# Sorted experts: back transfers issued twelve iterations ahead, a group of results every two and a half blocks

## The chip, the core and the metric

The kernel runs on one core of a Trainium2 chip. Its engines are TensorE (PE: matmuls and transposes, PEld its weight loads), VectorE (DVE), ScalarE (ACT), GpSimd (POOL) and SyncE (SP, which here only issues transfers). Each runs its own instructions in the order of its program and waits on semaphores for the others. The metric is the device time in microseconds; lower is better. A profiled execution gives a trace of one run.

## What is computed

A decoder layer for 64 sequences of 128 tokens of width 128, in f32: linear attention, attention over a context of 120 tokens, and a mixture of experts, each followed by a normalisation. The change lies in the third part:

```python
logits = x @ gate_w.T;  scores = softmax(logits)
topk_w, topk_i = top_k(scores, 2)
topk_w = topk_w / (topk_w.sum(-1) + 1e-20) * 2.5
...
g = silu(x @ w_gate[e]) * (x @ w_up[e])        # 8 experts, width 176
y = sum over the token's two experts of  topk_w * (g @ w_down[e])
y = y + (silu(x @ sw_gate) * (x @ sw_up)) @ sw_down     # shared expert, width 352
x = layernorm(x + y)
```

## The kernel before

During the second part the tokens' rows are sorted by expert into `sorted_rows` in device memory, once for sequences 0 to 47 and once for 48 to 63 (`PER = (48, 16)`). The last stage, `experts` (line 1420), then works through `TOTAL` = 142 blocks of 128 sorted rows, 103 of the first batch (`FIRST_BLOCK[1]` = 103) and 39 of the second. It is one loop over iterations t, which each engine's program runs through for itself; block i passes through it in stages:

- TensorE transposes the rows of block t (`turn_rows`), multiplies block t-1 with its expert's gate and up weights (`gate_up`), transposes the hidden rows of t-2 and projects t-3 down.
- ScalarE casts the transposed rows (`hi`), applies silu (`gate`) and copies hidden rows out (`turn`).
- VectorE forms the low part (`lo` of t), the product with the row's weight (`product` of t-1) and copies the result of t-3 out (`take`).
- GpSimd scatters the result of block t-3 into `sorted_results` in device memory, each row to its token's place (`scatter`, line 1595).
- SyncE loads the rows of blocks, three blocks at a time (`load_rows`): at its iteration t (a multiple of 3) those of blocks t+12 to t+14. For that it waits until the results of blocks t to t+2 have been scattered and landed, since the rows' buffers also hold the scatter's indices. `x_rows` (in the trace `w_wkv`) has 12 buffers. The last rows are loaded in iteration 129.

The shared expert is worked into the same loop for 16 groups of four sequences, in eight pieces a group from iteration 8 on; piece 0 to 2 of a group are its gate and up products, pieces 3 to 6 its projections. Groups 14 and 15 come after the blocks, from iteration 143 on, in seven pieces each (`LATE_FROM = TOTAL + 1`). `add_shared` adds a group's result to its rows in `X`.

When all blocks of the first batch are scattered, the results of its tokens can be fetched back: groups g = 0 to 11 (`WHOLE` = 12) while blocks 103 to 141 still run, groups 12 to 15 after the last block. `BACK_TIME[g]` is the iteration of a group's addition, and all its steps stand relative to it (first number for g < 12, second for the others):

- `load_back`: two transfers of 256 KB (a token's two expert results) into one of five `back` buffers, at -5 on SyncE. It waits for the sum of group g-5 (`BACKS` = 5). For g = 12, 13 it is at iteration `TOTAL + 5` on SyncE, for g = 14, 15 at `TOTAL + 11` on ScalarE, each behind a wait for the last scatter (`sent_after`).
- `add_pair` (line 1602), GpSimd, at 0: waits for both transfers and adds the two halves.
- `add_back` (line 1749), VectorE, at +1: waits for `add_pair` and `add_shared`, adds `X`, starts the statistics; `moments` at +2 ends them.
- `root` (line 1609), GpSimd, at +4 or +3; `shifts`, VectorE, at +5 or +4.
- `normalise` (line 1665), ScalarE, at +6 and +7, or +5 and +6: two activations each into one of four `result` buffers (`DEEP` = 4); the first waits until the store of group g-4 has landed.
- `store` (line 1549), SyncE, at +8 or +7: 256 KB to the output.

What sets the order is therefore the iteration in which a step is written; within an iteration an engine does its block's work first, and GpSimd the scatter, then `root`, then `add_pair`. SyncE does `load_rows`, then `load_back`, then `store`.

Of the kernel before, what the change touches and what calls it, by code (L numbers as in the profile page):

```python
# [155 lines left out]
FIRST_BLOCK = [sum(BLOCKS[:n]) for n in range(BATCHES + 1)]  # L156
TOTAL = FIRST_BLOCK[BATCHES]
# [7 lines left out]
GROUPS = B // GROUP  # L165
# [1254 lines left out]
def experts(nc, X, ident, later, slots, out):  # L1420
# [11 lines left out]
    LATE = 2  # L1432
    LATE_FROM = TOTAL + 1
    WHOLE = FIRST[1] // GROUP
    BACK_TIME = [FIRST_BLOCK[1] + 9 + 3 * g if g < WHOLE else TOTAL + 13 + 2 * (g - WHOLE) for g in range(GROUPS)]
    STEPS_ALL = BACK_TIME[-1] + 9
    CLOSE_AT = 30
    TABLE_AT = 10
# [3 lines left out]
    with ExitStack() as stack:  # L1442
# [72 lines left out]
        def prepared_at(t):  # L1515

            starts = [SHARED_FROM + PIECES * g for g in range(GROUPS)]
            return starts.index(t) if t in starts else None

        def back_at(t, *delays):  # L1520

            for g, start in enumerate(BACK_TIME):
                if t - start == delays[g >= WHOLE]:
                    return g
            return None

        @block.sync
        def _(sp):
# [24 lines left out]
            for t in range(STEPS_ALL):  # L1553
                if t % SET == 0 and t + RING < TOTAL:
                    load_rows(t // SET + LOADS)
                g = prepared_at(t + 13)
                if g is not None and g > 1:
                    load_all(g)
                if t == CLOSE_AT:
                    sp.wait_ge(slots.empty_ready, 6)  # L1560
                    sp.wait_ge(slots.table_ready, TABLE + 2)
                    slots.close_regions(sp, empty, 1)
                g = back_at(t, -5, -5)
                if g is not None and g < WHOLE:
                    if g == 0:
                        sent_after(sp, FIRST_BLOCK[1])
                    for c in range(2):
                        load_back(sp, g, c)
                if t == TOTAL + 5:
                    sent_after(sp, TOTAL)  # L1570
                    for g in (WHOLE, WHOLE + 1):
                        for c in range(2):
                            load_back(sp, g, c)
                g = back_at(t, 8, 7)
                if g is not None:
                    store(g)
# [49 lines left out]
        def _(act):  # L1626
# [42 lines left out]
            for t in range(STEPS_ALL):  # L1669
                if t < TOTAL:  # L1670
                    hi(t)
                if 0 <= t - 1 < TOTAL:
                    gate(t - 1)
                if 0 <= t - 2 < TOTAL:
                    turn(t - 2)
                g, k = shared_at(t)
                if g is not None and k < NS:
                    all_gate(g, k)
                g = prepared_at(t + 2)
                if g is not None:  # L1680
                    all_hi(g)
                if t == 1:
                    slots.turned_rows(act, ps_s, LAST)
                if t == 3:
                    slots.scores_of(act, LAST)
                for pair in range(2):
                    g = back_at(t, 6 + pair, 5 + pair)
                    if g is not None:
                        normalise(g, pair)
                if t == TOTAL + 11:  # L1690
                    sent_after(act, TOTAL)
                    for g in (WHOLE + 2, WHOLE + 3):
                        for c in range(2):
                            load_back(act, g, c)
# [237 lines left out]
```

## Time and profile before

| | |
|---|---|
| median of 3 runs | 2119.89 us (2117.36 to 2120.77) |
| profiled execution, whole | 2114.67 us |
| its span in the trace | 2112.9 us |
| TensorE busy over the span | 1958.9 us, 93% |
| VectorE, ScalarE, GpSimd busy | 72%, 60%, 63% |
| `experts`, first scatter to end of span | 1704.1 to 2112.9 us |
| additions of groups (`add_pair`) | 16, from 1969.6 to 2103.4 us |
| granted TensorE clock, whole span | 0.97 of full speed |

The shares are means over stages that differ. TensorE is over 90% busy up to the stretch in which the groups are added, and 50 to 60% in the last tenth of the span, so that stretch is read by itself: by the list of waits, and by the instructions in order of time, on each engine. A time in brackets behind an instruction is how long its engine stood idle before it, with the instruction or transfer that ended the wait.

### The profile page before, as it was taken

Reading aid. Unit: us, or ns where it says so; the run is one execution under the profiler, and the core shown is the slowest. Engines: PE = TensorE matmul, PEld = TensorE weight load, DVE = VectorE, ACT = ScalarE, POOL = GpSimd, SP = SyncE. Lnnn points to the kernel's source line nnn. Section 1 sums busy time; section 2 is a strip of 40 time slices with the busy share of each in tenths; the row PEclk is TensorE's granted clock in tenths of the full one; section 3 lists DMA queues with packets and bytes.
Section 4 is the critical chain, followed back from the end, with each engine's and each line's share of the span. In section 5 each row is a group of like instructions: output and inputs, shape, how many; then the busy total and the mean of one; then the engine's idle time right before and its main releaser. Section 6 shows DMA issues by size and latency. Waiting matters only on the chain. (4 is left out here: it accounts for less than half of the span.)

```text
span 2112.9 us, 47421 instructions
## 1 busy us (share of the span) xinstructions
PE 1958.9 (93%) x15991; PEld 1703.1 (81%) x15991; DVE 1527.1 (72%) x4046; ACT 1259.4 (60%) x3812; POOL 1336.8 (63%) x1459
## 2 busy tenths in 40 slices
PE   6888859999999999999999999999999999999655
PEld 4555449999999999999999999998999878888544
DVE  5999956777777777777777777778777655555445
ACT  3565536666666666666666666666666544444334
POOL 5899937666666666666666666666666654444445
PEclk9999979999999999999999999999999989999867
DMA  4200000000000000000000000001000122222335
GB/s 135 63 18 18 16 25 6 9 21 17 16 14 21 15 16 15 20 15 18 15 16 20 17 16 14 21 17 35 15 19 16 39 58 81 78 73 71 87 87 158
DMA packets 105022, 75.78 MB, mean 36 GB/s; under 512 B 11044, under 2 KB 98676, under 8 KB 104660
## 3 DMA queue, kind: packets, MB, share of 16 engines
q1 hardware_dynamic: 93732, 53.66, 9.1%
q0 software_dynamic: 8640, 17.97, 2.5%
q8 instruction: 135, 2.21, 0.4%
q10 hardware_dynamic: 2416, 1.12, 0.2%
q14 instruction: 99, 0.81, 0.1%
HBM read 40.15 MB, written 32.57 MB: 34 GB/s over the span
## 5 line engine op out<-in xcount | busy, mean ns | idle before, releaser
L1026 POOL TENSOR_TENSOR x_prob<-x_prob,x_inv 128x496 f32<-128x496 f32 x514 | 521.7, 1015 | 459.6 <-DVE x_inv L1176 457.0
L1104 ACT ACTIVATE x_prob<-x_ps_S,x_nmax 128x248 f32<-128x248 f32 x1028 | 472.8, 467 | 225.6 <-DVE x_nmax L1170 223.7
L1170 DVE TENSOR_REDUCE x_nmax<-x_ps_S 128x2 f32<-128x496 f32 x515 | 344.9, 670 | 105.1 <-PE x_ps_S L848 97.0
L1118 ACT COPY x_probT<-x_ps_T 124x512 f32<-124x512 f32 x512 | 300.3, 587 | 166.7 <-PE x_ps_T L1358 164.0
L846 PE MATMUL x_ps_S<-x_kT_lo,x_G_hi 128*128 128x248 f32 x1030 | 328.6, 319 | 0.0
L1358 PE MATMUL x_ps_T<-ident,x_prob 128*124 128x128 f32 x2048 | 319.0, 278 | 7.9 <-POOL x_prob L1026 6.4
L1358 PEld LDWEIGHTS x_ps_T<-ident,x_prob 128*124 128x124 f32 x2048 | 233.1, 140 | 74.1 <-POOL x_prob L1026 30.3
L848 PE MATMUL x_ps_S<-x_kT_hi,x_G_hi 128*128 128x248 f32 x1030 | 285.9, 278 | 0.0
L847 PE MATMUL x_ps_S<-x_kT_hi,x_G_lo 128*128 128x248 f32 x1030 | 285.5, 277 | 0.0
L1328 PE MATMUL x_ps_O<-x_probT,x_V 124*64 124x128 f32 x4096 | 251.9, 276 | 0.4 <-ACT x_probT L1118 0.4
L1595 POOL DMA_INDIRECT sorted_results<-e_y,w_wkv x142 | 149.2, 1051 | 158.9 <-DVE e_y L1719 149.2
L1156 DVE TENSOR_TENSOR x_G_lo<-x_ps_G,x_G_hi 128x512 fp32r<-128x512 f32 x259 | 177.9, 687 | 89.3 <-ACT x_G_hi L1098 89.1
L1328 PEld LDWEIGHTS x_ps_O<-x_probT,x_V 124*64 124x64 f32 x4096 | 221.0, 137 | 18.9 <-issue 5.2
L1104 ACT ACTIVATION_READ_ACCUMULATOR x_prob<-x_ps_S,x_nmax 128x1 f32 x1028 | 206.9, 201 | 0.0
L1098 ACT CAST x_G_hi<-x_ps_G 128x512 fp32r<-128x512 f32 x259 | 152.4, 589 | 74.5 <-PE x_ps_G L848 73.9
L847 PEld LDWEIGHTS x_ps_S<-x_kT_hi,x_G_lo 128*128 128x128 f32 x1030 | 195.7, 190 | 0.0
L846 PEld LDWEIGHTS x_ps_S<-x_kT_lo,x_G_hi 128*128 128x128 f32 x1030 | 194.8, 189 | 0.0
L848 PEld LDWEIGHTS x_ps_S<-x_kT_hi,x_G_hi 128*128 128x128 f32 x1030 | 194.1, 188 | 0.0
L1162 DVE COPY x_V<-x_ps_V 124x512 f32<-124x512 f32 x259 | 175.5, 678 | 2.6 <-PE x_ps_V L848 2.6
L281 POOL DMA_INDIRECT sorted_rows<-w_rows,slots_slot x128 | 132.3, 1034 | 27.9 <-issue 23.5
L847 PE MATMUL x_ps_G<-x_kT_hi,x_M_lo 128*128 128x256 f32 x518 | 146.3, 282 | 0.0
L846 PE MATMUL x_ps_G<-x_kT_lo,x_M_hi 128*128 128x256 f32 x518 | 146.0, 282 | 0.1
(240 smaller groups left out, 4491.1 us busy)
## 6 DMA issues: line engine op xcount, KB each, us to landing
w_wkv<-sorted_rows SPq DMA_DIRECT2D x142, 66.0 KB
e_back<-sorted_results SPq DMA_DIRECT2D x28, 256.0 KB, 3.5
x_nk<-latents SPq DMA_DIRECT2D x34, 124.0 KB
latents<-lin_nlat SPq DMA_DIRECT2D x32, 128.0 KB, 1.8
turned_rows<-w_rows SPq DMA_DIRECT2D x32, 128.0 KB, 1.7
w_wq<-turned_rows SPq DMA_DIRECT2D x32, 128.0 KB
out_dram<-e_result SPq DMA_DIRECT2D x16, 256.0 KB, 2.4
x_nk<-in_ctx SPq DMA_DIRECT2D x34, 120.0 KB, 2.3
```

The lines of the kernel that those rows point to most:

```text
L846: nc.tensor.matmul(out, stationary[0], moving[1], start=first, stop=False)
L847: nc.tensor.matmul(out, stationary[1], moving[0], start=False, stop=False)
L848: return nc.tensor.matmul(out, stationary[0], moving[0], start=False, stop=last)
L1026: nc.gpsimd.tensor_tensor(prob[:, k], prob[:, k], inv[:, k].unsqueeze(2).broadcast_to([P, 2, K]), ALU.mult).then_inc(prob_ready, 1)
L1098: nc.scalar.copy(G_part[0][:, pair], ps_G[:]).then_inc(G_hi_ready, 1)
L1104: nc.scalar.activation(prob[:, k, h, :], ps_S[:, n % BANKS, h * K:(h + 1) * K], ACT.Exp, bias=nmax[:, k, h:h + 1], accum_out=total[:, k, h ...
L1118: nc.scalar.copy(probT[0:KT, s % (2 * GANG)], ps_T[0:KT, s % 2, :]).then_inc(probT_ready, 1)
L1156: nc.vector.tensor_tensor(G_part[1][:, pair].rearrange("p h u q -> p (h u q)"), ps_G[:], G_part[0][:, pair].bitcast(F32).rearrange("p h u ...
L1162: nc.vector.tensor_copy(V[:, hf, u, tile, :], ps_V[0:KT, :]).then_inc(V_ready, 1)
L1170: nc.vector.tensor_reduce(nmax[:, k, :], ps_S[:, n % BANKS, 0:2 * K].rearrange("p (h k) -> p h k", h=2), AX, ALU.max, negate=True).then_in ...
L1328: last = nc.tensor.matmul(ps_O[h * DH:(h + 1) * DH, k * S:(k + 1) * S], V[:, j // 4, u, tile, (j % 4 * 2 + h) * DH:(j % 4 * 2 + h + 1) * D ...
L1358: last = nc.tensor.transpose(ps_T[0:KT, s % 2, at:at + S], prob[:, s % RINGS, h, tile * KT:(tile + 1) * KT], ident[:])
```

## The change

Four numbers change. `BACK_TIME` of the first twelve groups begins at iteration 115 instead of 112 and goes on by 2.5 iterations instead of 3 (115, 117, 120, 122, ... 142 instead of 112, 115, ... 145). That of the last four is 152, 154, 156, 158 instead of 155, 157, 159, 161. The transfers of the first twelve are issued twelve iterations ahead instead of five, so in SyncE's iterations 103, 105, 108, ... 130 instead of 107, 110, ... 140. ScalarE's transfers for groups 14 and 15 move from iteration 153 to 148. All steps that stand relative to `BACK_TIME` move with it. The loop ends after 167 iterations instead of 170.

```diff
-    BACK_TIME = [FIRST_BLOCK[1] + 9 + 3 * g if g < WHOLE else TOTAL + 13 + 2 * (g - WHOLE) for g in range(GROUPS)]
+    AHEAD = 12
+    BACK_TIME = [FIRST_BLOCK[1] + AHEAD + 5 * g // 2 if g < WHOLE else TOTAL + 10 + 2 * (g - WHOLE) for g in range(GROUPS)]
...
-                g = back_at(t, -5, -5)
+                g = back_at(t, -AHEAD, -AHEAD)
                 if g is not None and g < WHOLE:
...
-                if t == TOTAL + 11:
+                if t == TOTAL + 6:
                     sent_after(act, TOTAL)
```

GpSimd, around the first four additions, before. `sorted_results` is the scatter of a block, `e_back` the addition of a group, `e_rstd` its root:

```order
 L1595 DMA sorted_results<-e_y,w_wkv 20224x128 x104
 L1602 TENSOR_TENSOR e_back<-e_back 128x512
 L1595 DMA sorted_results<-e_y,w_wkv 20224x128 x3
 L1602 TENSOR_TENSOR e_back<-e_back 128x512
 L1595 DMA sorted_results<-e_y,w_wkv 20224x128
 L1609 TENSOR_TENSOR e_rstd<-e_vare,slots_half 128x4
 L1595 DMA sorted_results<-e_y,w_wkv 20224x128 x2
 L1602 TENSOR_TENSOR e_back<-e_back 128x512
```

The same place in the changed program (line numbers are one higher):

```order
 L1596 DMA sorted_results<-e_y,w_wkv 20224x128 x107
 L1603 TENSOR_TENSOR e_back<-e_back 128x512
 L1596 DMA sorted_results<-e_y,w_wkv 20224x128 x2
 L1603 TENSOR_TENSOR e_back<-e_back 128x512
 L1596 DMA sorted_results<-e_y,w_wkv 20224x128 x2
 L1610 TENSOR_TENSOR e_rstd<-e_vare,slots_half 128x4
 L1596 DMA sorted_results<-e_y,w_wkv 20224x128
 L1603 TENSOR_TENSOR e_back<-e_back 128x512
 L1596 DMA sorted_results<-e_y,w_wkv 20224x128
 L1610 TENSOR_TENSOR e_rstd<-e_vare,slots_half 128x4
```

The first addition stands three scatters later, and between two additions there are two and three scatters in turn instead of three.

SyncE, around the first store (of group 0), before. `w_wkv` are the rows of a block (here the last of three), `e_back` a group's pair of back transfers, `out_dram` a group's store:

```order
 L477 DMA w_wkv<-sorted_rows 128x132
 L1549 DMA out_dram<-e_result 128x4x128
 L1501 DMA e_back<-sorted_results 128x4x128 x2
 L476 TENSOR_LOAD slots_row_of
 L476 ISA x2
 L477 ISA
 L477 DMA w_wkv<-sorted_rows 128x132
```

The same place in the changed program:

```order
 L477 DMA w_wkv<-sorted_rows 128x132
 L1502 DMA e_back<-sorted_results 128x4x128 x2
 L1550 DMA out_dram<-e_result 128x4x128
 L1502 DMA e_back<-sorted_results 128x4x128 x2
 L1550 DMA out_dram<-e_result 128x4x128
 L476 TENSOR_LOAD slots_row_of
```

The store of group 0 was directly behind the rows of iteration 120; now it is in iteration 123, behind that iteration's rows and the pair of group 8, and the store of group 1 follows behind another pair ahead of the next rows.

VectorE, behind its last product of the shared expert (`e_all_hidden`), before. `e_hsum` is a group's sum, `e_stat`, `e_mom`, `e_vare` its statistics, `X` the last `add_shared`:

```order
 L1734 TENSOR_TENSOR e_all_hidden<-e_all_silu,e_ps_up 96x512
 L1749 TENSOR_TENSOR e_hsum<-e_back,X 128x512
 L1753 BN_STATS e_stat<-e_hsum 128x6 x2
 L1742 TENSOR_TENSOR X<-X,e_ps_s 128x512
 L1758 BN_STATS e_stat<-e_hsum 128x6 x2
 L1761 BN_AGGR e_mom<-e_stat 128x2 x4
 L1764 TENSOR_SCALAR e_vare<-e_mom 128x4
 L1749 TENSOR_TENSOR e_hsum<-e_back,X 128x512
```

The same place in the changed program:

```order
 L1735 TENSOR_TENSOR e_all_hidden<-e_all_silu,e_ps_up 96x512
 L1750 TENSOR_TENSOR e_hsum<-e_back,X 128x512
 L1754 BN_STATS e_stat<-e_hsum 128x6 x2
 L1759 BN_STATS e_stat<-e_hsum 128x6 x2
 L1762 BN_AGGR e_mom<-e_stat 128x2 x4
 L1765 TENSOR_SCALAR e_vare<-e_mom 128x4
 L1750 TENSOR_TENSOR e_hsum<-e_back,X 128x512
 L1754 BN_STATS e_stat<-e_hsum 128x6 x2
 L1759 BN_STATS e_stat<-e_hsum 128x6 x2
 L1762 BN_AGGR e_mom<-e_stat 128x2 x4
 L1765 TENSOR_SCALAR e_vare<-e_mom 128x4
 L1770 SCALAR_TENSOR_TENSOR e_shift<-e_mom,e_rstd 128x4
```

The last `add_shared` stood between the halves of group 12's statistics; now the whole of groups 12 and 13 stands ahead of it.

## Rows read from the trace of the kernel before

**Rows 1.** List of waits, 1680 us to the end: waiter <- awaited: us, times, longest.

```profile
PE e_ps_x L1808 <- DVE e_xT_lo L1703: 51.7, 25, 7.0
DVE e_hsum L1749 <- POOL e_back L1602: 45.0, 12, 6.4
POOL e_back L1602 <- DMA e_back<-sorted_results: 43.9, 11, 6.2
```

**Rows 2.** GpSimd in order of time: start, duration (us), line, out<-in, [idle before].

```profile
1969.61 1.26 POOL L1602 TENSOR_TENSOR e_back<-e_back 128x512 f32<-128x512 f32 x1 [5.79 <-DMA e_back<-sorted_results]
...
2018.98 1.42 POOL L1595 DMA_INDIRECT sorted_results<-e_y,w_wkv  x1 [0.16 <-issue]
...
2023.86 0.97 POOL L1595 DMA_INDIRECT sorted_results<-e_y,w_wkv  x1 [1.15 <-DVE e_y L1719]
2029.47 1.25 POOL L1602 TENSOR_TENSOR e_back<-e_back 128x512 f32<-128x512 f32 x1 [4.64 <-DMA e_back<-sorted_results]
...
2072.62 1.29 POOL L1602 TENSOR_TENSOR e_back<-e_back 128x512 f32<-128x512 f32 x1
...
2076.77 1.03 POOL L1595 DMA_INDIRECT sorted_results<-e_y,w_wkv  x1 [0.20 <-issue]
2078.10 0.97 POOL L1595 DMA_INDIRECT sorted_results<-e_y,w_wkv  x1 [0.30 <-issue]
2079.10 1.29 POOL L1602 TENSOR_TENSOR e_back<-e_back 128x512 f32<-128x512 f32 x1
```

**Rows 3.** Groups of instructions, 1968 to 2073 us: busy, mean ns, idle before.

```profile
L1602 POOL TENSOR_TENSOR e_back<-e_back 128x512 f32<-128x512 f32 x10 | 12.6, 1259 | 41.7 <-DMA e_back<-sorted_results 41.7
```

**Rows 4.** All engines in order of time: a block's first transpose, and one `take`.

```profile
1955.22 0.27 PE L1808 MATMUL e_ps_x<-ident,w_wkv 128*128 128x128 f32 x1
...
1957.35 0.29 DVE L1719 COPY e_y<-e_ps_y 128x128 f32<-128x128 f32 x1 [0.58 <-PE e_ps_y L1832]
...
1961.72 0.27 PE L1808 MATMUL e_ps_x<-ident,w_wkv 128*128 128x128 f32 x1
...
1964.69 0.28 PE L1808 MATMUL e_ps_x<-ident,w_wkv 128*128 128x128 f32 x1
...
2011.51 0.42 PE L1808 MATMUL e_ps_x<-ident,w_wkv 128*128 128x128 f32 x1
...
2013.88 0.42 PE L1808 MATMUL e_ps_x<-ident,w_wkv 128*128 128x128 f32 x1
```

**Rows 5.** Stretches: length, busy PE, PEld, DVE, ACT, POOL, then granted clock, DMA, GB/s.

```profile
2006.50:2011.00 4.50, 2.03 (x8) 1.80 (x9) 3.29 (x16) 0.68 (x3) 3.76 (x4) 0.50 0.05 16
...
2077.00:2084.00 7.00, 5.72 (x28) 3.81 (x26) 4.91 (x18) 4.05 (x9) 6.28 (x6) 1.00 0.22 69
2084.00:2098.00 14.00, 10.73 (x66) 8.27 (x66) 6.90 (x22) 6.13 (x15) 6.12 (x6) 1.00 0.67 196
```

**Rows 6.** SyncE's issues in order of time: rows of blocks, first store, pair of transfers.

```profile
2022.40 2.60 SPq L477 DMA_DIRECT2D w_wkv<-sorted_rows  x3
2025.04 0.43 SPq L1549 DMA_DIRECT2D out_dram<-e_result  x1
2025.52 1.12 SPq L1501 DMA_DIRECT2D e_back<-sorted_results  x2
```

**Rows 7.** From issue to landing: first the back transfers, then the stores.

```profile
DMA to landing us min/median/max: 2.8/3.6/5.2
...
DMA to landing us min/median/max: 2.2/2.4/5.0
```

**Rows 8.** ScalarE: first half of `normalise` of group 3, in iteration 127.

```profile
2022.61 0.88 ACT L1665 ACTIVATE e_result<-e_hsum,e_shift,e_rstd 128x128 f32<-128x128 f32 x2
```

**Rows 9.** VectorE in order of time, near the end.

```profile
2094.27 0.68 DVE L1749 TENSOR_TENSOR e_hsum<-e_back,X 128x512 f32<-128x512 f32 x1
...
2097.38 0.69 DVE L1742 TENSOR_TENSOR X<-X,e_ps_s 128x512 f32<-128x512 f32 x1 [1.91 <-PE e_ps_s L1859]
...
2104.69 0.69 DVE L1749 TENSOR_TENSOR e_hsum<-e_back,X 128x512 f32<-128x512 f32 x1
```

## The prediction, made before the changed kernel was run

> **What bounds the kernel now.** The list of waits comes first, for the last 430 us: I looked for one wait that three engines share. VectorE's sum of a group waits 45.0 us for GpSimd's addition of the two halves, in 12 waits; that addition itself waits 43.9 us for the transfer from `sorted_results`, in 11; and TensorE's transposes wait 51.7 us for VectorE [rows 1]. It is one queue of waits: the transfer is late, GpSimd stands, VectorE stands behind it in program order, so `lo` of the next block is late and TensorE runs dry.
>
> Next GpSimd in order of time [rows 2]. The addition of g = 0 stands 5.79 us, that of g = 5 4.64 us; of the ten additions up to 2073 nine stand so (g = 0 to 8), together 41.7 us [rows 3]. From 2072.62 on nothing stands: there the transfers were issued after SyncE's last rows of blocks, and GpSimd works without a gap. That stretch shows the next limit.
>
> Why the transfers are late, although issued "five iterations ahead": SyncE is not at the iteration of the others. `load_rows` at its iteration t waits until the scatter of block t+2 has landed, which GpSimd issues at t+5. So the transfer issued at 2025.52 belongs to the addition at 2029.47 [rows 2, 6], with no lead: the wait is its landing (2.8 to 5.2 us) [rows 7].
>
> Last the clock. In a stretch after a stall the granted clock is 0.50 (1.2 GHz), in stretches where TensorE is 77 to 82% busy it is 1.00 (2.4 GHz) [rows 5]. A block takes 2.37 us at the low level, TensorE without a gap (2011.51 to 2013.88) [rows 4].
>
> **The change, part by part.** *Transfers twelve iterations ahead.* The instructions are the same ones. Seven iterations more, at the 2.37 us of a block, are 16.6 us of lead against the 5.2 us of the longest landing. The waits of g = 0 to 8 go; what they cost is not their sum, since GpSimd then has less slack and the clock differs, so I build the new stretch up from its start.
>
> *Start.* Iterations 113 and 114 take 2.97 us each as before (1961.72 to 1964.69); iteration 115 starts at 1967.7. Its `take` follows 2.1 us later (1955.22 to 1957.35), the scatter some 0.6 us after that and lasts about 1 us, so the addition of g = 0, now in iteration 115, starts at about 1971.4 [rows 4].
>
> *Pace.* What is next late is GpSimd itself. From one addition to the next over three iterations it needs 6.48 us (2072.62 to 2079.10): addition, three scatters, one root [rows 2]. Over two iterations one scatter of 1.33 us goes (2076.77 to 2078.10): 5.2 us. TensorE needs at most 2.37 us for a block [rows 4], 5.9 us for the 2.5 blocks of a group even at the low clock, beside GpSimd's mean of 5.8. The additions stand in iterations 115, 117, 120, ... 142: five long gaps and six short, of which the first has no root and takes 5.2 - 1.2 = 4.0 us, two blocks of TensorE at some 2 us each. Sum: 5 x 6.48 + 5 x 5.2 + 4.0 = 62.4 us. Bounds: the scatter behind an addition takes 1.42 us and others 0.97 [rows 2]; were all eleven short, 5 us less (57.4). Were each block 2.6 us (the 2.37 of a low clock and some of VectorE's wait), 27 blocks are 70 us. I take 62.4, since its rows are the same instructions in the same order.
>
> *A new wait.* `normalise(g + 4)` overwrites the result buffer of g and waits for its store. It now stands 16 iterations behind BACK_TIME of g, before 18, while the store stays at +8 in SyncE's program, and SyncE is late as shown. The store of g = 0 is at SyncE's iteration 123, behind that iteration's rows and a pair of back transfers. From GpSimd's scatter of iteration 128: 3.42 us until SyncE passes its gate (2018.98 to 2022.40), 2.64 for three rows, 1.1 for the pair (rows of 1.12), then landing, 2.4 (median) to 5.0 us: 9.6 to 12.2 us [rows 2, 6, 7]. ScalarE reaches `normalise(4)` (iteration 131) 1.25 us before GpSimd's scatter there (2022.61 against 2023.86), so 6.48 - 1.25 = 5.2 us on that scale [rows 2, 8]. It waits 4.4 to 7.0 us. Behind it on ScalarE are `hi` of block 132 and `gate`, for which VectorE, TensorE and GpSimd wait: from the landing to the next scatter 2.4 us (two normalisations, `hi`, `lo`, `product`, `take`), so that scatter comes at 12.0 to 14.6 instead of 9.2: 2.8 to 5.5 us lost. I take 4. The store of g = 1 lands 1.6 us later and is wanted two iterations later: no wait. Those of g = 2 and 3 fall within 1 us of their need, and from g = 4 on SyncE has no gate. Below: 0, if the store's landing is shorter or blocks slower; above: 12, if three of the four wait.
>
> The store shares SyncE's queue with two 256 KB transfers just ahead of it. The Trainium skill (DMA: Bandwidth & Descriptors, section on queues, rings and completion order) says that one DMA engine takes a queue's descriptors in their order; by that the landing would be nearer 5.0 than 2.4 us, and the loss 5.5 rather than 2.8. No row before has a store directly behind such a pair with its own landing beside it.
>
> *Stretch of blocks together.* The addition of iteration 142 was at 2079.10; it comes at 1971.4 + 62.4 + 4 = 2037.8: 41.3 us earlier.
>
> *Tail.* From that addition to the end the order is nearly the old one. Before, VectorE ends its products at 2094.27, starts g = 12, waits 1.91 us for TensorE's last projection (2097.38), and only then does g = 12's rest and g = 13, until g = 15's sum at 2104.69 [rows 9]. Now g = 12 and 13 stand ahead of that wait and fill it: 2 us less. ScalarE's four transfers now stand ahead of the last gates: 4 issues of some 0.5 us, but the normalisations of g = 11 that stood there in part are done earlier; nothing either way. Bounds: -4 (the rest of the chain is also VectorE's) and +2 (the issues delay the gates). I take -2.
>
> *Edits at nothing:* transfers for g = 0 to 3 fall into iterations 103 to 112; SyncE has idle time there and their rows are wanted more than five iterations later. The five back buffers: the transfer of g waits for the sum of g - 5, 11.5 iterations ahead of its own addition; SyncE comes there some seven ahead. If SyncE were not gated, it would wait an iteration and a half.
>
> **Sum.** 41.3 + 2 = 43.3 us. The profiled execution took 2114.67 us (span 2112.9 and 1.8 around it); it would take 2071.4. The three timed runs have their median at 2119.89, 5.2 above; I count from the median: 2119.9 - 43.3 = 2076.6, so 2077 us. Extremes: 57.4, no store wait, -4 give 2066; 70, 12, +2 give 2096.
>
> **Rivals.**
> *The clock stays low.* GpSimd as the bound leaves TensorE idle for a part of every group; for it: behind a stall the clock was still 0.50 during the next blocks. Against it: 1.00 at 77% busy [rows 5]. Then the pace is the 70 us of above: 2084; with another store wait 2090. The Trainium skill (TensorE: Matmul & The Clock Gate, section "A second HAM failure mode: psum-queue depth-cycling") tells of a kernel whose clock swings because of frequent short idles; by that rule it would come out so.
> *No store wait.* If the first store lands within 5 us of SyncE's gate, or blocks are slower there, the 4 us stay: 2073.
> *Several store waits* (three at 4 us): 2085.
> *It does not do what it says.* If SyncE stood more than 12 iterations behind, the transfers would still be waited for: 2120. Against it: the gate is at five iterations and landing.
> *Slower: SyncE becomes the bound.* Between two gates it issues three rows (2.6 us), 1.2 pairs and 1.2 stores. If rows land late, TensorE starves in every third block. Before, three blocks took 109.5 / 10 = 10.9 us (addition 0 to 10); the kernel gets slower once SyncE needs more than that per three blocks, for instance 11.3: 2124. Its rows give 2.64 + 1.2 x (1.12 + 0.43) = 4.5 us [rows 6].
>
> **How the numbers follow.** Forecast (one store wait, GpSimd's pace, 2075 to 2080) 0.60; low clock 0.14; several store waits 0.08; no store wait or scatters all short (2066 to 2073) 0.12; no effect 0.03; slower 0.03. Predicted 2077. The range of 8 in 10 leaves out the last two, the slowest part of the low clock and the fastest of the fourth: 2068 to 2091. A measurement of this kernel tells 0.2%, some 4 us, from no change. Faster 0.94, same 0.03, slower 0.03.
>
> **What the new profile would show.** Right: no wait of the additions for the transfer until g = 11; GpSimd at 5.8 us a group and over 85% busy in iterations 117 to 142; the clock at 1.00 there; one idle stretch of ScalarE of 4 to 7 us ahead of a normalisation of g = 4; the pieces of g = 13 ahead of the last `add_shared`. Wrong: the additions still stand; the clock's mean in that stretch under 0.8; TensorE or VectorE without a gap while GpSimd waits; rows of blocks waited for by TensorE. The least certain steps are the pace and the size of the store wait.

## The result

The changed kernel takes 2084.47 us (median of 4 runs, 2082.94 to 2085.23) against 2119.72 us of the kernel before in the same session (median of 4): ratio 0.9834, 95% interval 0.9817 to 0.9851. That is 35.3 us less, inside the range and 7.5 us above the 2077 predicted. The profiled execution of the changed kernel took 2083.88 us (span 2081.9).

The line numbers after the change are one higher. In these first lines (list of waits, 1680 us to the end: waiter <- awaited: us, times, longest), those that answer to [rows 1] are the first three:

```profile
PE e_ps_x L1809 <- DVE e_xT_lo L1704: 18.3, 25, 5.0
POOL e_back L1603 <- DMA e_back<-sorted_results: 8.7, 2, 6.1
DVE e_hsum L1750 <- POOL e_back L1603: 7.2, 7, 2.1
ACT e_result L1666 <- DMA out_dram<-e_result: 5.9, 2, 5.1
```

The queue of waits is gone: 43.9 us in 11 waits of GpSimd for the transfers are now 8.7 in 2, TensorE's 51.7 us are 18.3. The last line is new: ScalarE waits for a store, as forecast.

GpSimd of the changed kernel in order of time, answering to [rows 2] (start, duration, line, out<-in, [idle before]): the additions of g = 0, 6, 10, 11, 12 and 13, and between them what follows on that of g = 6:

```profile
1977.23 1.29 POOL L1603 TENSOR_TENSOR e_back<-e_back 128x512 f32<-128x512 f32 x1
...
2010.65 1.19 POOL L1596 DMA_INDIRECT sorted_results<-e_y,w_wkv  x1 [1.09 <-DVE e_y L1720]
...
2016.35 1.29 POOL L1603 TENSOR_TENSOR e_back<-e_back 128x512 f32<-128x512 f32 x1
2017.81 1.43 POOL L1596 DMA_INDIRECT sorted_results<-e_y,w_wkv  x1 [0.17 <-issue]
2019.26 1.04 POOL L1610 TENSOR_TENSOR e_rstd<-e_vare,slots_half 128x4 f32<-128x4 f32 x1
2023.39 1.03 POOL L1596 DMA_INDIRECT sorted_results<-e_y,w_wkv  x1 [3.09 <-DVE e_y L1720]
...
2045.41 1.29 POOL L1603 TENSOR_TENSOR e_back<-e_back 128x512 f32<-128x512 f32 x1
2050.62 1.30 POOL L1603 TENSOR_TENSOR e_back<-e_back 128x512 f32<-128x512 f32 x1
2062.94 1.29 POOL L1603 TENSOR_TENSOR e_back<-e_back 128x512 f32<-128x512 f32 x1 [6.08 <-DMA e_back<-sorted_results]
2066.86 1.27 POOL L1603 TENSOR_TENSOR e_back<-e_back 128x512 f32<-128x512 f32 x1 [2.63 <-DMA e_back<-sorted_results]
```

No addition up to g = 11 stands. Those of g = 12 and 13, whose transfers can only start behind the last block, still do. The addition of g = 11 (iteration 142) is at 2050.62; the forecast on the scale of the profile of before was 2037.8. Here the two executions have to be laid side by side with care. SyncE's first pair of back transfers, the first instruction that the change moves, is at 1962.81 us after. A scatter of GpSimd well ahead of it (iteration 99, below called the common scatter) is at 1933.15 us before and the same one at 1938.20 after, and the rows that SyncE issues behind it at 1933.26 and 1938.31. The 5.0 us between them belong to the executions, not to the change: the profiled execution of before was 5.2 us under its own median. Counted from there, the addition of iteration 142 is 7.8 us later than forecast, and the rest is in these stretches (length, busy PE, PEld, DVE, ACT, POOL, granted clock, DMA share, GB/s; each from one addition to the next, the last is all eleven):

```profile
1981.74:1989.82 8.08, 6.23 (x34) 4.11 (x33) 7.44 (x25) 3.54 (x11) 5.52 (x5) 1.00 0.38 110
...
2016.35:2024.45 8.10, 3.10 (x16) 2.40 (x15) 3.44 (x14) 2.64 (x9) 4.78 (x4) 0.85 0.76 221
2024.45:2032.98 8.53, 7.82 (x37) 7.15 (x37) 6.49 (x24) 4.71 (x16) 5.50 (x5) 0.55 0.50 143
...
2045.41:2050.62 5.21, 4.74 (x28) 3.80 (x27) 4.10 (x17) 4.02 (x11) 4.79 (x4) 0.96 0.25 77
```

```profile
1977.23:2050.62 73.39, 55.27 (x289) 45.15 (x289) 52.40 (x203) 39.41 (x120) 55.47 (x48) 0.84 0.52 151
```

The eleven gaps are 4.51, 8.08, 6.13, 7.29, 5.05, 8.06, 8.10, 8.53, 5.21, 7.22 and 5.21 us. The last row above is a gap as forecast: 5.2 us with GpSimd 4.79 busy, 92%. The gaps of three iterations are not: 7.2 to 8.5 us with some 5.6 of GpSimd, where 6.48 were forecast. One gap of two iterations (2016.35 to 2024.45) holds the wait for the store.

The end, VectorE in order of time, answering to [rows 9]: the last product of the shared expert, the sums of g = 12 and 13, the last `add_shared`, the sum of g = 15:

```profile
2065.41 0.68 DVE L1735 TENSOR_TENSOR e_all_hidden<-e_all_silu,e_ps_up 96x512 f32<-96x512 f32 x1 [1.08 <-PE e_ps_up L848]
2066.01 0.68 DVE L1750 TENSOR_TENSOR e_hsum<-e_back,X 128x512 f32<-128x512 f32 x1
...
2068.16 0.69 DVE L1750 TENSOR_TENSOR e_hsum<-e_back,X 128x512 f32<-128x512 f32 x1
...
2070.98 0.68 DVE L1743 TENSOR_TENSOR X<-X,e_ps_s 128x512 f32<-128x512 f32 x1
...
2073.77 0.68 DVE L1750 TENSOR_TENSOR e_hsum<-e_back,X 128x512 f32<-128x512 f32 x1
```

Both sums stand ahead of `add_shared`, which no longer waits for TensorE (1.91 us before). From the last scatter of a block to the end it takes 28.1 us instead of 29.7.

### The profile page after: what moved, and what is told of

The parts are those of the page before. It is cut to its first block and busy times, and to the rows that moved or that the text cites. A ratio compares the mean times of both kernels' runs of the same rounds, so it can differ in the third digit from the quotient of the medians.

```text
span 2081.9 us, 47421 instructions
## 1 busy us (share of the span) xinstructions
PE 1955.8 (94%) x15991; PEld 1695.4 (81%) x15991; DVE 1532.7 (74%) x4046; ACT 1261.6 (61%) x3812; POOL 1338.7 (64%) x1459
## 5 line engine op out<-in xcount | busy, mean ns | idle before, releaser
L848 PE MATMUL x_ps_G<-x_kT_hi,x_M_hi 128*128 128x256 f32 x518 | 146.3, 282 | 0.0
```

The source lines that it names most:

```text
L848: return nc.tensor.matmul(out, stationary[0], moving[0], start=False, stop=last)
```

## The experiments

Each was compared with the kernel before in its own session, whose median was 2119.7 us for the whole change, 2117.7 for the next four, 2117.6 for the four behind them and 2118.9 for the last four. Kernels of different sessions are therefore compared by their ratios, not by their medians. "Distance" is the time from the addition in iteration 115 to that in 142, in the profiled execution; "tail" is from the last scatter of a block to the end. Both are of one execution. How far a distance varies between executions can be seen once: two of the kernels run the same program up to iteration 147 (transfers ahead alone, and the same with the new tail), and from g = 0 to g = 11 they take 76.6 and 78.5 us. A difference of 1 or 2 us in one distance shows nothing by itself.

| kernel | median us | ratio, 95% interval | tail us |
|---|---|---|---|
| the whole change | 2084.5 | 0.9834 (0.9817 to 0.9851) | 28.1 |
| transfers ahead alone | 2072.4 | 0.9789 (0.9773 to 0.9805) | 29.6 |
| closer additions and new tail alone | 2126.9 | 1.0048 (1.0031 to 1.0065) | 28.1 |
| whole, eps on ScalarE | 2080.5 | 0.9825 (0.9809 to 0.9841) | 28.1 |
| whole, stores two iterations earlier | 2079.1 | 0.9818 (0.9801 to 0.9834) | 29.4 |
| transfers ahead and new tail | 2073.2 | 0.9790 (0.9774 to 0.9807) | 29.9 |
| whole, more transposes | 2080.7 | 0.9827 (0.9811 to 0.9844) | 28.2 |
| whole, eps and stores | 2078.2 | 0.9814 (0.9798 to 0.9831) | 30.9 |
| transfers ahead, new tail, more transposes | 2072.1 | 0.9790 (0.9774 to 0.9806) | 29.1 |
| lead seven | 2116.5 | 0.9989 (0.9979 to 1.0000) | 29.7 |
| lead eight | 2075.1 | 0.9788 (0.9768 to 0.9807) | 29.6 |
| whole, eps, stores of g up to 9 | 2078.5 | 0.9802 (0.9782 to 0.9821) | 28.7 |
| transfers ahead, more transposes | 2077.4 | 0.9799 (0.9777 to 0.9820) | 29.6 |

### The two parts apart

First the transfers nine iterations ahead (in SyncE's iterations 103, 106, ...; the first pair is then in iteration 103, as in the whole change), additions and tail as before. This and the diffs below are against the changed kernel, unless said otherwise:

```diff
-    BACK_TIME = [FIRST_BLOCK[1] + AHEAD + 5 * g // 2 if g < WHOLE else TOTAL + 10 + 2 * (g - WHOLE) for g in range(GROUPS)]
+    BACK_TIME = [FIRST_BLOCK[1] + 9 + 3 * g if g < WHOLE else TOTAL + 13 + 2 * (g - WHOLE) for g in range(GROUPS)]
...
-                g = back_at(t, -AHEAD, -AHEAD)
+                g = back_at(t, -9, -9)
...
-                if t == TOTAL + 6:
+                if t == TOTAL + 11:
```

> One part alone: the back transfers are issued nine iterations ahead (in iterations 103, 106, ...), but BACK_TIME of all groups and the tail are those of the kernel before. Theory (the lead of the transfers is the gain; the pace of 2.5 blocks a group only loads GpSimd and VectorE more): no addition waits for its transfer (four iterations more lead at 2.4 us, against a landing of at most 5.2), normalise waits for no store (18 iterations behind), a group takes 6.5 to 7.3 us per three blocks, so the addition of iteration 142 comes 41 to 46 us earlier than before; total 2073 to 2080, below the changed kernel's 2084.5. Rival (the closer pace carries a part of the gain): 2088 to 2100.

Measured 2072.4 us, ratio 0.9789 against 0.9834 of the whole change: 9 to 10 us less than that, and of all kernels here only one comes as low (2072.1, below). From the common scatter to the end it takes 135.8 us, the whole change 143.7, the kernel before 179.8. Then the closer additions and the new tail, with the transfers five ahead as before:

```diff
-                g = back_at(t, -AHEAD, -AHEAD)
+                g = back_at(t, -5, -5)
```

> The other part alone: the new BACK_TIME (115, 117, 120, ... and the late four), with the back transfers still five iterations ahead. Theory: the additions go on waiting 3 to 6 us each for their transfers, nearly no gain in the stretch of blocks, 2 us in the tail: 2112 to 2122. Rival (the pace carries a part of the gain): 2095 to 2108.

Measured 2126.9 us, 0.48% slower than before, and slower than the 2112 to 2122 us expected. The waits of the two, the additions' in each (1680 us to the end), ahead alone first, closer additions second:

```profile
POOL e_back L1603 <- DMA e_back<-sorted_results: 2.5, 2, 1.8
```

```profile
POOL e_back L1603 <- DMA e_back<-sorted_results: 60.8, 10, 8.5
```

So the change is two changes of unlike sign. The lead is worth -45.3 us (2117.7 to 2072.4), the closer additions with the new tail +9.2 with the transfers five ahead, and +10 (-45.3 to -35.3) once the lead is there. That the two prices are nearly alike is chance, for they are not the same loss. With the transfers five ahead the additions stand 60.8 us instead of the 43.9 of before. SyncE passes the gate of its iteration t only behind GpSimd's iteration t+5, and the transfers of g = 3 and 4, now in SyncE's iterations 117 and 120, are let go in iterations 122 and 125, those of their own additions: these stand 8.5 us each. With the lead no addition stands, and the loss lies elsewhere (below). In the same 27 iterations (115 to 142) the kernel with the lead alone takes 63.0 us and the whole change 73.4. The first of these, by the view of stretches (columns as above):

```profile
1973.40:2036.40 63.00, 50.32 (x286) 39.41 (x285) 43.14 (x181) 36.85 (x116) 51.88 (x46) 0.92 0.60 172
```

There GpSimd is 82% busy, VectorE 68%, with nine groups added in the stretch; after the change the same iterations hold eleven.

### The store wait

SyncE of the changed kernel in order of time: rows of three blocks, pair of g = 8, store of g = 0, pair of g = 9; then ScalarE's first instruction of `normalise(4)`:

```profile
2014.19 2.39 SPq L477 DMA_DIRECT2D w_wkv<-sorted_rows  x3
2016.59 0.94 SPq L1502 DMA_DIRECT2D e_back<-sorted_results  x2
2017.58 0.51 SPq L1550 DMA_DIRECT2D out_dram<-e_result  x1
2018.13 1.30 SPq L1502 DMA_DIRECT2D e_back<-sorted_results  x2
```

```profile
2021.23 0.88 ACT L1666 ACTIVATE e_result<-e_hsum,e_shift,e_rstd 128x128 f32<-128x128 f32 x2 [5.08 <-DMA out_dram<-e_result]
```

The store of g = 0 is issued at 2017.58 and ScalarE goes on at 2021.23. Does it cost what its wait says? All stores of g < 12 two iterations earlier (that of g = 0 at SyncE's iteration 121, behind an earlier gate):

```diff
-                g = back_at(t, 8, 7)
+                g = back_at(t, 6, 7)
```

> The changed kernel, with the stores of the first twelve groups two iterations earlier in SyncE's program (+6 instead of +8), so that group 0's stands ahead of the gate of iteration 123. Theory (normalise of g = 4 waits 5.1 us for that store, and about 3 of it is lost): the wait is gone, 2.5 to 4 us less, 2080.5 to 2082. Rival (the time is given back to GpSimd's queue): within 1 us of 2084.5.

Measured 2079.1 us, below the 2080.5 to 2082 expected; the interval of its ratio overlaps that of the whole change, so the size is read from the trace. ScalarE's longest wait for a store is 1.1 us instead of 5.1, and the distance is 69.6 instead of 73.4 us: the wait was worth 3.8 us. But the tail gave back 1.3, since the addition of g = 12 waited 9.0 us instead of 6.1. The store of g = 10 now stands in SyncE's iteration 146, and there waits for ScalarE's `normalise(10)`, with the transfers of g = 12 and 13 (iteration 147) queued behind it.

### The eps addition

The gap of 8.08 us has no store wait and a full clock. VectorE (7.44 us busy of 8.08) and GpSimd there, one instruction of each:

```profile
1981.30 1.75 DVE L1765 TENSOR_SCALAR e_vare<-e_mom 128x4 f32<-128x4 f32 x1
```

```profile
1981.74 1.27 POOL L1603 TENSOR_TENSOR e_back<-e_back 128x512 f32<-128x512 f32 x1
```

Adding eps to four numbers a partition takes 1.75 us instead of the 0.17 or 0.37 that it takes in eight others of this stretch. By its row it ends at 1983.05, and GpSimd's addition at 1983.01. The same stands at 2007.75 (1.85 us; addition 2008.29 to 2009.57) and 2023.94 (1.83; 2024.45 to 2025.73). The Trainium skill (SBUF — State Buffer, section "Who interferes with whom") says that a `tensor_scalar` of VectorE can enter a mode in which it needs the pair of ports that it shares with GpSimd, and that the later of two such instructions is blocked until the other ends; the ends agree with that. The starts in the trace are those of VectorE, 0.44 to 0.54 us ahead of GpSimd's, so which of the two had the ports first the trace does not tell. Nor does it tell whether this instruction, whose input has a stride, was in that mode. With the additions three iterations apart the eps falls elsewhere: nine of them take 1.7 us together in the lead alone, eleven take 7.6 in the whole change.

Moved to ScalarE, as an activation with a bias:

```diff
-                v.tensor_scalar(vare[:, g % DEEP], mom[:, g % DEEP, :, 1], EPS, None, ALU.add).then_inc(vare_ready, 1)
...
+                    nc.scalar.activation(vare[:, g % DEEP], mom[:, g % DEEP, :, 1], ACT.Identity, bias=eps[:, 0:1], scale=1.0
+                                         ).then_inc(vare_ready, 1)
```

> The changed kernel, with the addition of eps to the variances (L1765, on VectorE, between two SBUF tensors) done by ScalarE as an activation with a bias instead. In the changed kernel this small instruction lasts 1.75 to 1.85 us where it meets GpSimd's addition of a pair (3 of 12) and 0.17 to 0.37 elsewhere. Theory (VectorE stands there until GpSimd's instruction ends, and TensorE's next block behind it): the three long ones go, the long gaps between additions fall from 8.1 to 7 us, total 3 to 6 us less, 2078 to 2081. Rival (the pace is lost to TensorE's clock alone, which stays low in half the stretch): within 1.5 us of 2084.5.

Measured 2080.5 us, distance 72.7: the gap of 8.08 us became 7.29, the other two with such an eps, 8.06 and 8.53, became 8.30 each, where 7 was expected. The interval overlaps that of the whole change, so what is shown is the 0.8 us of the gap, not the 4 us between the medians. The first long gap shows it again and again: 8.08 to 8.09 us in the three kernels at this pace and with this lead that have eps on VectorE, 7.27 to 7.55 in the three that have it on ScalarE.

Both together (the diffs of the two last):

> The changed kernel with both single repairs: eps added by ScalarE, stores at +6. Alone the second brought the distance of the additions from 73.4 to 69.6 us, the first to 72.7, with other store waits in its place. Theory (the two losses are separate, VectorE's stands cost 1 to 1.6 us each and were hidden in the first run by longer store waits): 65 to 67.5 us, total 2074.5 to 2077.5. Rival (what a repaired stand gives is taken back by the queue of GpSimd): 69 to 70 us, 2079.

Measured 2078.2 us; distance 68.5, above the 65 to 67.5 expected: 1.1 less than with the stores alone, and 4.9 less than the whole change. A gap of two iterations and one of three, in it:

```profile
2012.59:2017.79 5.20, 3.58 (x21) 2.60 (x20) 3.50 (x16) 3.16 (x11) 4.79 (x5) 0.93 0.78 214
2017.79:2025.20 7.41, 6.93 (x34) 6.04 (x33) 4.73 (x20) 4.28 (x14) 5.74 (x6) 0.59 0.72 195
```

The short gaps are GpSimd's (4.79 of 5.20). The long ones stay at 7.2 to 8.2 us with 5.5 to 5.7 of GpSimd. The tail is 30.9 us. The addition of g = 12 in it:

```profile
2059.23 1.27 POOL L1606 TENSOR_TENSOR e_back<-e_back 128x512 f32<-128x512 f32 x1 [10.17 <-DMA e_back<-sorted_results]
```

To see if the store of g = 10 is the reason, the same with the stores of g = 10 and 11 at +8 again:

```diff
-                g = back_at(t, 8, 7)
-                if g is not None:
-                    store(g)
+                for late in (0, 1):
+                    g = back_at(t, 8 if late else 6, 7)
+                    if g is not None and late == (g >= WHOLE - 2):
+                        store(g)
```

> The whole change with the stores at +6 only for groups 0 to 9 and at +8 for 10 and 11 (eps on ScalarE as in the run with both). The run with all twelve at +6 lost 2.8 us in the tail, where the store of group 10 stood in SyncE's iteration 146 ahead of the last groups' transfers in 147. If that is the reason, the tail (last scatter to end) is 28.1 again instead of 30.9, the addition of group 12 waits 6 us and not 10, the distance of the additions 115 to 142 stays 68.5, and the time is 2075.5 us (0.980 to 0.981). If the tail stays long, the reason is another (ScalarE's load), and the time is 2078.

```profile
2057.61 1.29 POOL L1607 TENSOR_TENSOR e_back<-e_back 128x512 f32<-128x512 f32 x1 [5.51 <-DMA e_back<-sorted_results]
```

The wait is 5.51 us again and the tail 28.7 instead of 30.9 (28.1 were expected): the reason is shown. The time, 2078.5 us in a session whose before was 1.2 us slower, has a ratio of 0.9802 against 0.9814, with intervals that overlap; the 2 us are seen in the trace and not in the runs. From the common scatter to the end it takes 139.6 us: of the 8 us between the whole change (143.7) and the lead alone (135.8) the stores and eps give back 4.1, and some 4 stay.

### The new tail

Lead alone with the new tail (and ScalarE's transfers at iteration 148):

```diff
-    BACK_TIME = [FIRST_BLOCK[1] + AHEAD + 5 * g // 2 if g < WHOLE else TOTAL + 10 + 2 * (g - WHOLE) for g in range(GROUPS)]
+    BACK_TIME = [FIRST_BLOCK[1] + 9 + 3 * g if g < WHOLE else TOTAL + 10 + 2 * (g - WHOLE) for g in range(GROUPS)]
...
-                g = back_at(t, -AHEAD, -AHEAD)
+                g = back_at(t, -9, -9)
```

> The first twelve groups every three blocks from iteration 112 with transfers nine ahead (as in the run of the lead alone), and the changed kernel's times for the last four groups and ScalarE's transfers. Theory (VectorE does g = 12 and 13 ahead of its wait for the last projection, worth 2 us, whatever the pace before): 1 to 3 us below the lead alone, 2070 to 2072 beside 2072.4. Rival (the tail's gain was the earlier end of g = 11, which is at 145 again here): equal within 1 us.

Measured 2073.2 us, ratio 0.9790 against 0.9789: no gain. With g = 11 at iteration 145, its predecessors' normalisations and ScalarE's four transfers meet ahead of the last gates. ScalarE and TensorE in order of time:

```profile
2047.12 0.39 ACTq L1502 DMA_DIRECT2D e_back<-sorted_results  x1
...
2047.56 2.03 ACTq L1502 DMA_DIRECT2D e_back<-sorted_results  x3
...
2051.04 0.50 PE L846 MATMUL e_ps_gate<-e_all_lo,w_shared_gate_hi 128*128 128x512 f32 x1 [3.26 <-ACT e_all_silu L1657]
```

TensorE waits 3.26 us for ScalarE's gate, which stands behind these issues; with the lead alone the same matmul waits 1.43. So the reason that the prediction gave for its upper bound of the tail ("the issues delay the gates") came true at the other pace.

### The clock

The granted clock over the distance was 0.84, not 1.00. To raise it without touching another engine, TensorE got four more transposes a block in iterations 117 to 141, into a part of PSUM that is overwritten before it is read:

```diff
+                if FILL_FROM <= t < TOTAL:
+                    if t == FILL_FROM:
+                        pe.wait_ge(all_silu_ready, (GROUPS - LATE) * NS)
+                    for n in range(FILL):
+                        nc.tensor.transpose(ps_gate[:, 0:P], ident[:], ident[:])
```

> The changed kernel with four more transposes of the identity (about 0.5 us, into a bank that nothing reads) behind each block's work on TensorE in iterations 117 to 141, whose only purpose is that TensorE idles less. Measured without them: clock 0.84 of full speed between the additions of iterations 115 and 142, which lie 73.4 us apart. Theory (a part of the 11 us above the forecast pace is the clock that falls in TensorE's idle pieces): the clock rises over 0.92 there and the distance falls by 2 to 5 us. Rival (VectorE and GpSimd set the pace, the clock only follows): the clock rises, the distance stays within 1.5 us or grows by up to 5, since a late block starts 0.5 us later.

```profile
1974.27:2048.17 73.90, 60.51 (x390) 50.57 (x390) 51.97 (x203) 39.82 (x120) 55.41 (x48) 0.93 0.52 150
```

The clock is 0.93 instead of 0.84 and the distance 73.9 instead of 73.4 us. (The intervals of the ratios overlap; from the common scatter to the end it takes 144.4 us, the whole change 143.7.) But two other things changed in that distance. ScalarE's wait for the store of g = 0 is 6.3 us instead of 5.1, and the transposes are work themselves: TensorE is busy for 60.51 us instead of 55.27. Two of the long gaps of this run, that of iterations 127 to 130 and the one from 132 to 135:

```profile
2005.40:2013.08 7.68, 6.58 (x48) 5.36 (x48) 6.53 (x25) 4.43 (x14) 5.49 (x5) 1.00 0.41 121
...
2022.38:2030.75 8.37, 8.37 (x50) 7.66 (x50) 6.69 (x25) 5.04 (x16) 5.50 (x5) 0.71 0.45 130
```

The first took 8.06 us at a clock of 0.79 in the changed kernel, and 7.68 at 1.00 here. In the second TensorE is busy from end to end. The same transposes in the kernel with the lead and the new tail, and in that with the lead alone:

> The kernel of three blocks a group with the new tail, and the four extra transposes of the fill run. Clock 0.92 in its stretch without them. Theory (GpSimd's 6.48 us per three blocks is the floor, 7.1 was measured, the rest is clock): 1 to 4 us below the same kernel without the fill. Rival (the chain TensorE, ScalarE, VectorE of a block sets it): equal or up to 4 us slower.

> Transfers nine ahead alone (2072.4), with four more transposes a block for TensorE in iterations 117 to 141, which write to a part of PSUM that is overwritten before it is read; additions, last groups and ScalarE's transfers as in the kernel before. With the new tail the same transposes gave 1.0 us (2073.2 to 2072.1) and a granted clock of 1.00 instead of 0.91 over the additions 112 to 142. Theory: the low clock costs 1 to 3 us at the three-block pace: 2069.5 to 2071.5. Rival, the clock is without effect there, since GpSimd and VectorE set the pace: 2072 to 2073.

The first of these took 2072.1 us, against 2073.2 without them in the same session, with a stretch from the first to the last addition (g = 0 to 11) of 75.8 us at a clock of 1.00, against 78.5 at 0.91. The second took 2077.4, against 2075.1 of the lead of eight in the same session and 2072.4 of the lead alone in another. The second expectation is missed: not faster. Nor do the transposes make it slower: the profiled execution's common scatter is 4.7 us later than that of the lead alone, ahead of all transposes, and from there to the end it takes 135.5 us against 135.8. Its stretch, below it that of the same kernel without the transposes, and that of the lead of eight:

```profile
1969.71:2045.92 76.21, 67.58 (x455) 54.90 (x453) 53.29 (x217) 43.83 (x133) 60.56 (x54) 1.00 0.56 164
```

```profile
1965.05:2041.61 76.56, 61.98 (x355) 48.29 (x353) 53.72 (x217) 43.50 (x133) 60.88 (x54) 0.93 0.57 164
```

```profile
1967.52:2043.06 75.54, 60.87 (x355) 45.72 (x353) 53.41 (x217) 43.36 (x133) 60.75 (x53) 0.98 0.57 166
```

At this pace the stretch is 76.2 and 75.8 us at a clock of 1.00, 75.5 at 0.98, and 76.6 and 78.5 at 0.93 and 0.91: no effect that is clear of the 1.9 us between two executions of one program. What is shown is that a full clock does not bring the gaps to the 6.48 us of the forecast: in the kernel with the new tail and the transposes, with 1.00 in every gap, the nine from iteration 115 to 142 take 6.46 to 7.70 us, 6.9 in the mean. What the low clock costs at the closer pace is not shown. The run that raised it gave TensorE more work, and in the changed kernel's gap at 0.55 TensorE is busy for 7.82 of the 8.53 us.

### The lead in steps

The prediction rests on SyncE's gate: `load_rows` at the iterations 105, 108, ... waits for the scatters of three blocks. If so, the lead counts by gates, not by iterations. Seven ahead puts a pair into iteration 105, behind the same gate as the 107 of five ahead; eight ahead puts it into 104, behind the gate before. All else as in the lead alone (diff against that kernel):

```diff
-                g = back_at(t, -9, -9)
+                g = back_at(t, -7, -7)
```

> The lead in steps. As the run that moved only the transfers (nine iterations ahead, additions, last groups and ScalarE's transfers as in the kernel before), but seven iterations ahead. SyncE passes its gates at the iterations 105, 108, ... ; with seven ahead a pair stands in iteration 105, 108, ..., with five ahead (the kernel before) in 107, 110, ...: behind the same gate, only the store of an older group changes place with it. Gate theory: the two iterations are worth nothing but the store's 0.4 us a group: ten waits of 3.5 to 4.5 us stay, the time is 2112 to 2118 us (ratio 0.997 to 1.000). Rival, the lead counts by iterations (two of them at 2.4 us are 4.8 us, the mean wait of before was 4.2): the waits all but go, 2075 to 2085 us.

and with `-8`:

> The same with eight iterations ahead: the pair stands in iteration 104, 107, ..., which is behind the gate before. Gate theory: one iteration more than the run with seven gives the whole gain, 2071 to 2076 us, as nine ahead (2072.4); no addition up to group 8 waits for its transfer. Rival, by iterations: one step of 2.4 us a group from the run with seven, that is no more than 10 x 2.4 = 24 us between the two.

Seven: 2116.5 us, 0.9989. Eight: 2075.1 us, 0.9788. One iteration is worth 41.4 us, the two before it 2.4. In the traces, the waits of the additions (1680 us to the end), seven first and then eight:

```profile
POOL e_back L1603 <- DMA e_back<-sorted_results: 38.9, 11, 5.0
```

```profile
POOL e_back L1603 <- DMA e_back<-sorted_results: 2.8, 3, 1.5
```

SyncE with seven ahead, rows of three blocks and the pair, and GpSimd's next addition:

```profile
2006.23 2.67 SPq L477 DMA_DIRECT2D w_wkv<-sorted_rows  x3
2008.92 0.93 SPq L1502 DMA_DIRECT2D e_back<-sorted_results  x2
```

```profile
2012.98 1.25 POOL L1603 TENSOR_TENSOR e_back<-e_back 128x512 f32<-128x512 f32 x1 [4.41 <-DMA e_back<-sorted_results]
```

The same with eight ahead:

```profile
2002.95 2.58 SPq L477 DMA_DIRECT2D w_wkv<-sorted_rows  x3
...
2006.05 1.14 SPq L1502 DMA_DIRECT2D e_back<-sorted_results  x2
```

```profile
2003.93 1.29 POOL L1603 TENSOR_TENSOR e_back<-e_back 128x512 f32<-128x512 f32 x1
...
2010.61 1.28 POOL L1603 TENSOR_TENSOR e_back<-e_back 128x512 f32<-128x512 f32 x1
```

With seven, the pair is issued at 2008.92 and the very next addition stands 4.41 us for it. With eight, the additions at 2003.93 and 2010.61 do not stand. The pair at 2006.05 is that of the second, 4.6 us ahead of it: just enough for the landing (2.8 to 5.2 us before), and the addition behind it does stand, for 0.86 us. The theory that every iteration of lead is worth a block's time is refuted.

## Why the prediction was right, and where it was off

- **What bounds the kernel: right.** Late transfers in one queue of waits, late because SyncE is gated. The lead alone gives 45 us; the step of one iteration at the gate shows the reason.
- **The time:** inside the range of 2068 to 2091, but outside the 2075 to 2080 that the forecast's own account had for itself, and at the 2084 of a rival. Of a gain of 43.3 us forecast, 35.3 came.
- **The lead: right conclusion, wrong measure.** "Seven iterations more, at the 2.37 us of a block" counts iterations; from five ahead on, two more were worth 2.4 us in all, the third 41.4. Twelve is beyond the gate: the pair of g = 8 was issued at 2016.59, its addition came at 2032.98.
- **Counting from the median: right.** The profile of before was an execution 5 us under its median; the changed kernel's was 0.6 under its own.
- **Start: right.** Addition of g = 0 forecast at 1971.4, found at 1977.23 less the 5.04 us, 1972.2.
- **Store wait: right, also in its parts.** SyncE passed its gate 3.54 us behind the scatter of iteration 128 (2010.65 to 2014.19; forecast 3.42), the store was landed 10.6 us behind it (9.6 to 12.2), ScalarE stood 5.08 us (4.4 to 7.0), the scatter of iteration 132 came at 12.7 us (12.0 to 14.6), and taking the wait away gave 3.8 us (4). A second wait, of `normalise(7)`, was 0.8 us.
- **Pace: the term that was mis-sized.** 62.4 us were forecast; without the store wait it is 69.6. With 73.4 in the place of 66.4 it is 7.0 of the 8 us missing. The short gaps were as forecast (5.0 to 5.2, one 6.1, the first 4.5 instead of 4.0). The five long ones were 6.48 each by the forecast and are 7.2 to 8.2 even in the kernel with eps and stores mended, together 37.2 instead of 32.4. The 6.48 came from one place, 2072.62 to 2079.10 in the trace of before, and there the blocks run out: of their stages only the last ones are left. The groups of instructions of before between 2072 and 2080 us have one `lo` of VectorE beside four scatters, where three blocks in full flow have three. "The same instructions in the same order" held for GpSimd alone:

```profile
L1595 POOL DMA_INDIRECT sorted_results<-e_y,w_wkv x4 | 4.4, 1098 | 1.7 <-DVE e_y L1719 1.1 <-issue 0.7
...
L1703 DVE TENSOR_TENSOR e_xT_lo<-e_ps_x,e_xT_hi 128x128 fp32r<-128x128 f32 x1 | 0.3, 274 | 0.0
```

  The kernel with the lead alone shows the same: its nine gaps of three iterations from 115 to 142 take 7.0 us in the mean, and the last of them 6.46. About 1 us of what is missing is VectorE's eps standing at GpSimd's addition (69.6 to 68.5, and the gap of 8.08). What makes up the other 6 us, 4.8 of them in the long gaps, stays open. A full clock does not make three iterations 6.48 us (above), but that the low one has no part in it is not shown either. In the long gaps with eps and stores mended GpSimd is busy for 5.5 to 5.7 us, VectorE for at most 81% of them, and TensorE for 65 to 94%, the most in the gap of 7.41 us at a clock of 0.59. A candidate beside the clock is the round through the engines: in the kernel with eps and stores mended, VectorE's eleven sums of the stretch stand 8.4 us for GpSimd's additions (groups of instructions, 1974 to 2043 us), with a block's `lo` queued behind each. That it sets the pace is argued, not tried.

```profile
L1761 DVE TENSOR_TENSOR e_hsum<-e_back,X 128x512 f32<-128x512 f32 x11 | 7.6, 688 | 8.4 <-POOL e_back L1606 8.4
```

- **"GpSimd over 85% busy, the clock at 1.00": wrong.** 76% and 0.84. The bound "each block 2.6 us, 70 us" was the better value (69.6 without the store wait); whether for its reason, a low clock and some of VectorE's wait, is open.
- **Tail: size near, reason half.** From the addition of iteration 142 to the end 31.3 us instead of 33.8, forecast -2. It needs the closer additions: at the old pace the new tail gave nothing. "From 2072.62 on nothing stands" was not so for g = 12 and 13, which waited 0.93 and 1.25 us for their transfers before and 6.08 and 2.63 after.
- **The rivals.** The low clock gives the right time (2084, with 70 us of pace; 69.6 were measured) and the clock did fall, to 0.84. That it was the cause is not shown: the run at 0.93 had the same distance, but more work for TensorE and a longer store wait in it. It is not the whole cause: the gap of 8.08 us was at a clock of 1.00, and at the old pace three iterations at 1.00 took 6.9 us, not 6.48. Several store waits: a second of 0.8 us, no more. SyncE did not become the bound.
- **Not seen at all:** that the closer pace itself costs. The prediction asked what the addition of iteration 142 gains against before; it did not ask what the lead gives with the additions left where they were. The price of the second part was never a term of the sum, so the sum could not show that one part of the change was a loss of 8 to 10 us.

## What to carry to other kernels

A prefetch behind a gated queue has its lead counted in gates: find the gate that it stands behind, and moving it by one iteration across that gate may be worth all, moving it by two on the near side nothing. Run each part of a change by itself, and price it also against the kernel in which the wait is gone: packing the groups closer cost 10 us there, for other reasons than the 9 it cost beside the wait. A pace read from a place where other work has already ended is a lower bound, not the value (6.48 us there, 7.0 in the mean of the stretch).

## What the runs showed of the hardware

A VectorE `tensor_scalar` over 128x4 numbers took 1.75 to 1.85 us instead of 0.17 or 0.37 where a GpSimd addition over 128x512 started half a microsecond behind it, and ended with it (three times in the changed kernel). On ScalarE the same addition took 0.30 us, and the gap between two additions of GpSimd in which it lay became 0.8 us shorter; in the kernel's time this was not clear of the noise.
